# Setup of a 32-batch DiT block on one core: one block of setup before the loop against setup steps with slots of their own

## The chip, the cores and the metric

The kernel runs on one core of one Trainium2 chip. The metric is the device time of one execution in microseconds (us). Before the change three runs took 1508.64, 1509.5 and 1513.65 us, median 1509.5 us. The kernel is written for the five engines directly: TensorE (PE), VectorE (DVE), ScalarE (ACT), GpSimd (POOL) and SyncE (SP), which here issues every DMA. Each engine works through its own list of instructions in program order and waits on semaphores.

## The reference

One transformer block with modulation and cross attention, for 32 batches of 256 tokens, width 256, 16 heads of 16, context of 256 tokens, MLP width 1024, all in fp32:

```python
c_proj = silu(c) @ W_mod + b_mod                    # 32 x 1536, once for all batches
shift_a, scale_a, gate_a, shift_m, scale_m, gate_m = split(c_proj, 6)
qkv = (ln(x) * (1 + scale_a) + shift_a) @ W_qkv + b_qkv
x = x + gate_a * (self_attention(qkv) @ W_proj + b_proj)
x = x + cross_attention(ln(x) @ W_qc + b_qc, ln(context) @ W_kvc + b_kvc) @ W_cproj + b_cproj
h = gelu((ln(x) * (1 + scale_m) + shift_m) @ W_mlp1 + b_mlp1) @ W_mlp2 + b_mlp2
return x + gate_m * h
```

## The kernel before, in words

**Batches and slots.** The work is cut into 32 batches. A table `PLAN` (L34) gives every step of a batch a lag, a half and a slot; `moment` (L99) makes one slot number of it, less what `AHEAD` (L66) says. 32 slots are one batch in the steady state. Each engine walks through all slots in order, and in a slot it does the steps that are its own (its function `at`). The order of the instructions on an engine is therefore written out by hand; when they run is decided by semaphores alone. Slot 0 is the one in which the first row maxima of batch 0 are due: four matmuls `max_ps` (L661) on PE, one reduction `mx_self` (L1015) on DVE. Slots below 0 hold what comes before: `load_x` and `ln1` of batch 0 at slot -44, `norm1` (POOL) at -44, the turn `t1` at -32, `q` at -26, `q_hi` and `q_lo` at -24, `k` at -14, `stack_q` at -11, `stack_k` and `k_lo` at -10, `v` at -5; of batch 1 `load_x` at -11, `ln1` at -8, `norm1` at -2.

**Precision.** Weights and activations are split into two fp16 parts, hi and lo; each product is three matmuls (`three`, L346: L348, L349, L350). Hi is a copy on ACT (`split_weight` L755, instruction L759), lo is the difference on DVE (`split_weight` L893, instruction L897; for `mlp2` on POOL, L1123). For the weights that are stacked by heads the split is one instruction for each stripe: 17 for `qkv`, 9 for `kvc`, 8 for `qc`.

**Setup.** It stands ahead of the slots on every engine, in this order.

- SP (from L358): the DMAs of `cond`, `W_mod` (two halves of rows, L360 and L361), `b_mod` (L362), eight bias columns (L367), seven weights (L371: qkv, mlp1, kvc, proj, qc, cproj, mlp2), then bias rows and columns (L379 to L386). `load_x` (L407) comes in slot -44, so behind all of them.
- ACT: it waits for `cond`, `W_mod` and `b_mod` (`setup_in`), makes the exponential of `cond` (L763), then splits six weights.
- DVE: silu of `cond` (L887 to L889) and the copy cT (L891), then the lo parts of qkv, mlp1, kvc and proj, then the sum MOD = `c_proj` (L905), and only then the turned shifts and scales (L911 to L919) and the bias columns of q and k (L925).
- PE: the turn of silu (L529), six pairs of fp32 matmuls 128x512 for `c_proj` (L535), eight turns (L540), the folded bias of q and k.
- POOL: the identity, the fill of `k_stack_self` (L1115), the fill of V with ones (L1118).

`late_setup` stands at slot 0 on every engine and `last_setup` at slot 32 (`slots`, L152). Late setup: on DVE the lo parts of `qc` and `cproj`, the columns (L933 to L940), `v_bias` (L942), the columns of the MLP (L944), the folded rows (L947 to L955); on PE the matmuls between them, in `max_ps`, `o_ps` and `exp_ps`; on ACT the split of `mlp2`; on SP the rows out and back (L392 to L398), after all of it. PE's late setup starts with

```python
pe.wait_ge(w_lo_done, len(EARLY_W))   # L555
...
pe.wait_ge(dve_set, 12)
```

and ends with the second line: PE goes to slot 0 only when DVE has finished all of it. DVE's ends in the same way.

Of the kernel before, what the change touches and what calls it, by code (L numbers as in the profile page):

```python
# [89 lines left out]


# [13 lines left out]
class Timeline:  # L105


    def __init__(self, batches, kinds):
# [12 lines left out]
        assert len(self.steps) == batches * (len(PLAN) - 2 * len(kinds))  # L121
# [18 lines left out]
def block_kernel(nc, x, cond, ctx_in, W_mod, b_mod, W_qkv, b_qkv, W_proj, b_proj, W_qc, b_qc, W_kvc, b_kvc,  # L140
# [11 lines left out]
    def slots(at, late_setup, last_setup=None):  # L152

        for slot in range(line.first, line.last + 1):
            if slot == 0:
                late_setup()
            if slot == 2 * TILES and last_setup:
                last_setup()
            at(slot, lambda step: line.steps.get((step, slot)))

    with ExitStack() as stack:
# [103 lines left out]
        bias_in = sem("bias_in")  # L265
        setup_in, w_in = sem("setup_in"), [sem(f"w_in_{i}") for i in range(4)]
        w_hi_done, w_lo_done, late_in = sem("w_hi_done"), sem("w_lo_done"), sem("late_in")

        zeroed, ident_zero, ident_made, consts = sem("zeroed"), sem("ident_zero"), sem("ident_made"), sem("consts")
        pe_set, dve_set, act_set, sp_set = sem("pe_set"), sem("dve_set"), sem("act_set"), sem("sp_set")  # L270
# [23 lines left out]
        def flat(t):  # L294
# [8 lines left out]
        EARLY_W = W_ORDER[:-1]  # L303
        w_wait = {"qkv": (0, 16), "mlp1": (1, 16), "kvc": (2, 64), "proj": (2, 64), "qc": (2, 64), "cproj": (2, 64),
                  "mlp2": (3, 16)}

# [50 lines left out]
        def _(sp):  # L357
            nc.sync.dma_start(cnd, cond).then_inc(setup_in, 16)  # L358
# [3 lines left out]
            nc.sync.dma_start(b_mod_rows, bass.AP(tensor=b_mod.tensor, offset=0, ap=[[0, NB], [1, 6 * D]])  # L362
                              ).then_inc(setup_in, 16)
            for n in range(2):
                for a in range(2):
                    for c in range(C):
                        nc.sync.dma_start(b_qk_col[64 * a:64 * a + 64, n * C + c:n * C + c + 1], stacked_bias(b_qkv, n * D, a, c)  # L367
                                          ).then_inc(bias_in, 16)

            def load_weight(name):  # L370
                nc.sync.dma_start(staged[name], w_dram[name].rearrange("(k p) n -> p k n", p=P)  # L371
                                  ).then_inc(w_in[w_wait[name][0]], 16)

            for name in W_ORDER[:4]:
                load_weight(name)
            for name in W_ORDER[4:]:
                load_weight(name)
# [9 lines left out]
            sp.wait_ge(zeroed, 1)  # L387

            def late_setup():

                sp.wait_ge(dve_set, 12)
                nc.sync.dma_start(rows_a_dram[:, 0], MOD[:, 2 * D:3 * D]).then_inc(sp_set, 16)  # L392
                nc.sync.dma_start(rows_b_dram[:, 0], MOD[:, 5 * D:6 * D]).then_inc(sp_set, 16)
                nc.sync.dma_start(rows_a_dram[:, 1], gb_a).then_inc(sp_set, 16)
                nc.sync.dma_start(rows_b_dram[:, 1], gb_m).then_inc(sp_set, 16)
                nc.sync.dma_start(bc_dram, bc_row[0:1]).then_inc(sp_set, 16)
                sp.wait_ge(sp_set, 16 * 5)
                nc.sync.dma_start(bc_rows[:], bass.AP(tensor=bc_dram.tensor, offset=0, ap=[[0, P], [1, D]])).then_inc(sp_set, 16)  # L398
# [16 lines left out]
            def load_rows(b, dst, src, s):  # L415
                row = src[b.n:b.n + 1].rearrange("a r d -> a (r d)")
                nc.sync.dma_start(dst[:, b.u].rearrange("p r d -> p (r d)"), row.to_broadcast([P, 2 * D])
                                  ).then_inc(s[b.u], 16)

            def do_stack(b, n):  # L420

                kind = QKV_OF[n]
                if kind == "cross" and b.n == 0:
                    sp.wait_ge(consts, 3)
# [30 lines left out]
            def o_gather(b, kind):  # L455

                sp_wait(o_recip[kind], b.n)
                sp_wait(o_copied[kind], b.n * 4 + 4)
# [33 lines left out]
            def at(slot, due):  # L492
                if (b := due("load_x")):
                    load_x(b)
# [24 lines left out]
            slots(at, late_setup)  # L519
# [5 lines left out]
        def _(pe):  # L525
            pe.wait_ge(ident_made, 1)
# [4 lines left out]
            pe.wait_ge(dve_set, 2)  # L531
            for i in range(3):
                dst = (max_ps, max_ps, exp_ps)[i][0:NB, i % 2]
                for c in range(C):
                    mm = pe.matmul(dst, cT[:, c], (wm, wm2)[c][:, i * 512:(i + 1) * 512], start=c == 0, stop=c == C - 1)  # L535
            mm.then_inc(pe_set, 1)
            pe.wait_ge(dve_set, 3)
            for i, part in enumerate((0, 1, 3, 4)):
                for c in range(C):
                    mm = pe.transpose(dense_ps[:, 1, (2 * i + c) * NB:(2 * i + c + 1) * NB],  # L540
                                      MOD[:, part * D + c * P:part * D + (c + 1) * P], ident[0:NB, 0:NB])
            mm.then_inc(pe_set, 1)
            pe.wait_ge(dve_set, 5)
            pe.wait_ge(w_lo_done, 1)
            sh = lambda part, lo, c: shT[:, lo, 2 * part + c]
            for m in range(2 * C):
                for c in range(C):
                    w = slice(m * P, (m + 1) * P)
                    mm = three(pe, dense_ps[:, 0, m * NB:(m + 1) * NB], w_hi["qkv"][:, c, w], w_lo["qkv"][:, c, w],
                               sh(0, 0, c), sh(0, 1, c), c == 0, c == C - 1)  # L550
            mm.then_inc(pe_set, 1)
            pe.wait_ge(dve_set, 6)

            def late_setup():
                pe.wait_ge(w_lo_done, len(EARLY_W))  # L555
                for m in range(FC):
                    for c in range(C):
                        w = slice(m * P, (m + 1) * P)
                        three(pe, max_ps[:, 0, m * NB:(m + 1) * NB], w_hi["mlp1"][:, c, w], w_lo["mlp1"][:, c, w],
                              sh(1, 0, c), sh(1, 1, c), c == 0, c == C - 1)  # L560
                for c in range(C):
                    w = slice(2 * D, 3 * D)
                    mm = three(pe, max_ps[0:NB, 1, 0:D], sh(0, 0, c), sh(0, 1, c), w_hi["qkv"][:, c, w],
                               w_lo["qkv"][:, c, w], c == 0, c == C - 1)
                mm.then_inc(pe_set, 1)
                pe.wait_ge(dve_set, 8)
                for c in range(C):
                    pe.transpose(o_ps[:, 0, c * NB:(c + 1) * NB], v_bias[:, c * P:(c + 1) * P], ident[0:NB, 0:NB]
                                 ).then_inc(pe_set, 1)
                for c in range(C):  # L570
                    mm = three(pe, exp_ps[0:NB, 0, 0:D], vcT[:, 0, c], vcT[:, 1, c], w_hi["cproj"][:, c],
                               w_lo["cproj"][:, c], c == 0, c == C - 1)
                mm.then_inc(pe_set, 1)
                pe.wait_ge(dve_set, 10)
                for c in range(C):
                    mm = three(pe, exp_ps[0:NB, 1, 0:D], vbT[:, 0, c], vbT[:, 1, c], w_hi["proj"][:, c],
                               w_lo["proj"][:, c], c == 0, c == C - 1)
                mm.then_inc(pe_set, 1)
                pe.wait_ge(dve_set, 12)

            def last_setup():
                pe.wait_ge(consts, 2)
# [7 lines left out]
            def turn(b, unit, k):  # L590

                pe.wait_ge(norm_step[k], b.n * 3 + 3)
                ps = tenant(b, unit)
                for c in range(C):
# [5 lines left out]

# [611 lines left out]
```

## Time and profile before

| | |
|---|---|
| three runs, us | 1508.64, 1509.5, 1513.65 |
| the profiled execution, us | 1505.56 |
| its span, us | 1503.3 |
| mean granted TensorE clock | 0.972 |
| PE busy | 1380.9 us, 92% |
| DVE, ACT, POOL busy | 74%, 73%, 47% |
| first row maximum on DVE (slot 0) | 52.7 us |

The profiled execution took 1505.56 us for a span of 1503.3 us, so 2.3 us lie around the span. It is 3.9 us below the median of the three runs. The shares of busy time are means over the whole span; the change touches its first 55 us.

### The profile page before, as it was taken

The numbers are of one execution on the slowest core, as the hardware profiler recorded it, in microseconds if no ns is written. First come the engines' busy times: TensorE is split into PE (matmuls) and PEld (weight loads), VectorE is DVE, ScalarE is ACT, GpSimd is POOL, SyncE is SP. The second block draws the span as 40 slices with busy tenths as digits, with TensorE's granted clock in tenths as the row PEclk, the third lists the DMA queues.
The fourth block names the chain that finished last, engine by engine and source line by source line (L and its number), as shares of the span: only waits on it lengthen the run. The fifth ranks groups of instructions, "written<-read, shape, count | busy, mean of one in ns | idle before, by whom it ended". The sixth has DMA issues, their size and how long they took to land.

```text
span 1503.3 us, 39974 instructions
## 1 busy us (share of the span) xinstructions
PE 1380.9 (92%) x15090; PEld 910.1 (61%) x15090; DVE 1111.4 (74%) x1992; ACT 1094.2 (73%) x1852; POOL 705.6 (47%) x995
## 2 busy tenths in 40 slices
PE   2577899999999999999999999999999999999775
PEld 1234466666666666666666666666666666665544
DVE  4647887788777777788777788778777777775543
ACT  3244687777777888778778888778778888777551
POOL 2233344455545554455554554455554554445421
PEclk8779999999999999999999999999999999999988
DMA  5122233333323333333323323333333232322110
GB/s 178 50 72 87 88 94 96 97 106 101 99 91 99 89 97 98 96 105 105 99 91 100 91 91 101 97 100 109 96 95 97 90 96 95 99 91 67 52 50 15
DMA packets 142133, 137.97 MB, mean 92 GB/s; under 512 B 38070, under 2 KB 116567, under 8 KB 141943
## 3 DMA queue, kind: packets, MB, share of 16 engines
q1 hardware_dynamic: 141942, 135.42, 29.0%
q8 instruction: 121, 1.98, 0.6%
q14 instruction: 70, 0.57, 0.1%
HBM read 56.34 MB, written 9.55 MB: 44 GB/s over the span
## 4 chain that ended last, share of the span: by engine, by line
PE 77%; DVE 9%; DMA 4%; ACT 3%; issue 3%; POOL 2%; SPq 2%; DVEq 0%; ACTq 0%; POOLq 0%
PE dense_ps L348 15%; PE dense_ps L350 13%; PE dense_ps L349 13%; PE o_ps L696 13%; PE max_ps L661 10%; PE exp_ps L678 7%; PE dense_ps L596 4%; DVE mx_cross L1015 3%; DVE mx_self L1015 2%; DMA o_rb_cross<-r_dram_cross 2%; ACT probs L818 1%; SPq L433 1%; DMA r_dram_cross<-o_r_cross 1%; PE dense_ps L623 1%; POOL Y L1179 1%
## 5 line engine op out<-in xcount | busy, mean ns | idle before, releaser
L818 ACT ACTIVATE probs<-exp_ps 128x1024 f32<-128x1024 f32 x512 | 525.3, 1026 | 189.0 <-PE exp_ps L678 186.5
L1015 DVE TENSOR_REDUCE mx_cross<-max_ps 128x4 f32<-128x1024 f32 x256 | 313.4, 1224 | 101.8 <-PE max_ps L661 94.2
L1015 DVE TENSOR_REDUCE mx_self<-max_ps 128x4 f32<-128x1024 f32 x256 | 312.3, 1220 | 78.5 <-PE max_ps L661 76.4
L1150 POOL TENSOR_TENSOR o_n_self<-o_n_self,o_rb_self 128x512 f32<-128x512 f32 x32 | 40.5, 1266 | 292.9 <-DMA o_rb_self<-r_dram_self 292.9
L1183 POOL TENSOR_TENSOR g_split<-G,g_split 128x512 f16<-128x512 f32 x120 | 136.5, 1159 | 58.5 <-ACT g_split L807 58.5
L348 PE MATMUL dense_ps<-mlp_hi,g_split 128*128 128x256 f16 x504 | 140.2, 278 | 5.1 <-DVE g_split L1093 5.1
L348 PE MATMUL dense_ps<-xt,mlp_hi 128*128 128x256 f16 x512 | 140.8, 275 | 3.0 <-DVE xt L979 2.8
L349 PE MATMUL dense_ps<-xt,mlp_hi 128*128 128x256 f16 x512 | 140.5, 274 | 0.0
L350 PE MATMUL dense_ps<-xt,mlp_lo 128*128 128x256 f16 x512 | 140.4, 274 | 0.0
L350 PE MATMUL dense_ps<-mlp_hi,g_split 128*128 128x256 f16 x504 | 139.6, 277 | 0.0
L349 PE MATMUL dense_ps<-mlp_lo,g_split 128*128 128x256 f16 x504 | 139.5, 277 | 0.0
L696 PE MATMUL o_ps<-probs,V_self 128*32 128x256 f32 x2048 | 138.2, 388 | 0.0
L696 PE MATMUL o_ps<-probs,V_cross 128*32 128x256 f32 x2048 | 137.5, 386 | 0.2 <-ACT o_sb_cross L826 0.2
L849 ACT ACTIVATE G<-dense_ps,cols_b_all 128x256 f32<-128x256 f32 x256 | 103.6, 469 | 34.6 <-PE dense_ps L350 34.5
L661 PE MATMUL max_ps<-k_stack_self,q_stack_self 48*128 48x256 f16 x1024 | 101.6, 277 | 22.3 <-DVE mx_self L1015 17.3
L661 PE MATMUL max_ps<-k_stack_cross,q_stack_cross 48*128 48x256 f16 x1024 | 101.1, 276 | 21.5 <-DVE mx_cross L1015 19.3
L1141 POOL TENSOR_SCALAR xn<-X,nm,rs 128x256 f32<-128x256 f32 x192 | 105.6, 557 | 10.5
L1150 POOL TENSOR_TENSOR o_n_cross<-o_n_cross,o_rb_cross 128x512 f32<-128x512 f32 x31 | 39.4, 1270 | 151.1 <-DMA o_rb_cross<-r_dram_cross 151.1
L678 PE MATMUL exp_ps<-q_stack_self,k_stack_self 50*128 50x256 f16 x1024 | 100.1, 273 | 10.0 <-ACT probs L818 6.7
L678 PE MATMUL exp_ps<-q_stack_cross,k_stack_cross 50*128 50x256 f16 x1024 | 98.9, 270 | 8.3 <-ACT probs L818 7.7
L661 PEld LDWEIGHTS max_ps<-k_stack_cross,q_stack_cross 48*128 48x128 f16 x1024 | 29.4, 94 | 91.3 <-DVE mx_cross L1015 60.7
L696 PEld LDWEIGHTS o_ps<-probs,V_self 128*32 128x32 f32 x2048 | 53.7, 109 | 49.8 <-issue 28.0
(230 smaller groups left out, 3337.3 us busy)
## 6 DMA issues: line engine op xcount, KB each, us to landing
q_stack_self<-split_q SPq DMA_DIRECT2D x192, 64.0 KB, 2.6
k_stack_self<-split_k SPq DMA_DIRECT2D x192, 64.0 KB, 2.6
k_stack_cross<-split_kc SPq DMA_DIRECT2D x192, 64.0 KB, 2.6
q_stack_cross<-split_qc SPq DMA_DIRECT2D x192, 64.0 KB, 2.6
X<-in_x SPq DMA_DIRECT2D x32, 256.0 KB, 2.8
Ctx<-in_ctx SPq DMA_DIRECT2D x32, 256.0 KB, 3.2
rows_a<-rows_a_dram SPq DMA_DIRECT2D x32, 256.0 KB, 3.4
o_n_self<-o_sb_self SPq DMA_DIRECT2D x64, 128.0 KB, 2.8
```

Of the source, the lines that this page charges most:

```text
L348: eng.matmul(dst, a_hi, b_hi, start=first, stop=False)
L349: eng.matmul(dst, a_hi, b_lo, start=False, stop=False)
L350: return eng.matmul(dst, a_lo, b_hi, start=False, stop=last)
L661: mm = pe.matmul(max_ps[:, ab, qt * T:(qt + 1) * T], q_stack[kind][rows, b.u, p, qt * P:(qt + 1) * P], k_stack[kind][rows, b.u, p], start= ...
L678: mm = pe.matmul(exp_ps[:, ab, kt * T:(kt + 1) * T], k_stack[kind][rows, b.u, p, kt * P:(kt + 1) * P], q_stack[kind][rows, b.u, p], start= ...
L696: mm = pe.matmul(o_ps[32 * j:32 * j + 32, 0, (g % 2) * T:(g % 2 + 1) * T], V[kind][:, b.u, kt, 4 * g + j], probs[:, tile % 8, kt * T:(kt + ...
L818: nc.scalar.activation(probs[:, t % 8:t % 8 + 2], exp_ps[:], ACT.Exp).then_inc(exp_taken[kind], 2)
L849: last = nc.scalar.activation(G[:, f], bank(f"mlp1_{i}")[:, m * T:(m + 1) * T], ACT.Gelu_apprx_tanh, bias=cols_b_all[:, b.n, C + f:C + f + 1])
L1015: nc.vector.tensor_reduce(mx[kind][:, :, :, t // 2].rearrange("p q a -> p a q"), max_ps[:].rearrange("p a (q k) -> p a q k", q=2), AX_X, A ...
L1141: last = nc.gpsimd.tensor_scalar(xn[k][:, t], src[:, t], nm[k][:, t:t + 1], rs[k][:, t:t + 1], ALU.add, ALU.mult)
L1150: nc.gpsimd.tensor_tensor(o_n[kind][:], o_n[kind][:], o_rb[kind][:], ALU.mult).then_inc(o_mult[kind], 1)
L1183: nc.gpsimd.tensor_tensor(g_split[:, 1, 2 * i:2 * i + 2], G[:, 2 * i:2 * i + 2], g_split[:, 0, 2 * i:2 * i + 2], ALU.subtract).then_inc(g_ ...
```

## The change

Each setup step gets a name and a slot in a table `FOLD`, and each engine does it inside `at` like a step of a batch. `late_setup` and `last_setup` are gone. The diff, cut to its core:

```diff
+FOLD = {"mod_0": -43, "mod_0_out": -43, "mod_0_turn": -42, "mod_0_split": -42, "hi_qkv": -44, "lo_qkv": -41,
+        "q_bias": -30, "q_bias_out": -30, "hi_mlp1": -25, "hi_kvc": -13, "hi_proj": -12, "hi_qc": -12, "hi_cproj": -12, "hi_mlp2": -4,
+        "lo_mlp1": -10, "lo_kvc": -9, "lo_proj": -8, "lo_qc": -8, "lo_cproj": -7, "lo_mlp2": 1,
+        "mod_rest": -41, "mod_add": -29, "mod_turn": -25, "shift_split": -23, "columns": -9,
+        "shift": -4, "shift_out": -4, "row_v": -3, "row_v_out": -2, "row_c": -3, "row_c_out": -2, "gate": -1, "gate_out": -1,
+        "rows_out": 0, "row_back": 1, "k_ones": 33, "v_ones": -25}
@@ SP: W_mod in two parts, qkv and x early, no bias columns of q and k
-            nc.sync.dma_start(wm[:, 0:6 * D], wm_dram[:, 0]).then_inc(setup_in, 16)
-            nc.sync.dma_start(wm2[:, 0:6 * D], wm_dram[:, 1]).then_inc(setup_in, 16)
+            nc.sync.dma_start(wm[:, 0:2 * D], wm_dram[:, 0, 0:2 * D]).then_inc(mod_in, 16)
+            nc.sync.dma_start(wm2[:, 0:2 * D], wm_dram[:, 1, 0:2 * D]).then_inc(mod_in, 16)
+            load_weight("qkv")
+            nc.sync.dma_start(X[:, 0], x[0:1].rearrange("a (t p) d -> p (a t) d", p=P)).then_inc(x_in[0], 16)
             nc.sync.dma_start(b_mod_rows, bass.AP(tensor=b_mod.tensor, offset=0, ap=[[0, NB], [1, 6 * D]])
+                              ).then_inc(b_mod_in, 16)
+            nc.sync.dma_start(wm[:, 2 * D:6 * D], wm_dram[:, 0, 2 * D:6 * D]).then_inc(mod_rest_in, 16)
+            nc.sync.dma_start(wm2[:, 2 * D:6 * D], wm_dram[:, 1, 2 * D:6 * D]).then_inc(mod_rest_in, 16)
+            for name in W_ORDER[1:]:
                 load_weight(name)
-            sp.wait_ge(zeroed, 1)
@@ PE: 36 matmuls of the identity first, then steps
+            pe.wait_ge(ident_made, 2)
+            fill(o_ps[:, 0], 36)
             pe.wait_ge(dve_set, 1)
...
+            def mod_0():
+                pe.wait_ge(dve_set, 2)
+                pe.wait_ge(mod_in, 16 * 2)
+                for c in range(C):
+                    mm = pe.matmul(max_ps[0:NB, 0], cT[:, c], (wm, wm2)[c][:, 0:2 * D], start=c == 0, stop=c == C - 1)
+                mm.then_inc(pe_set, 1)
+            def mod_rest():
+                pe.wait_ge(mod_rest_in, 16 * 2)
...
+            def row_c():
+                pe.wait_ge(dve_set, dve_value["columns"])
+                pe.wait_ge(dve_set, dve_value["shift_out"])
+                pe.wait_ge(w_lo_done, w_turn("cproj"))
...
-                pe.wait_ge(dve_set, 12)
@@ PE: waits with their first reader (batch 0 only)
+                    pe.wait_ge(w_lo_done, w_turn(name))      # features_out, tokens_out
+                        pe.wait_ge(mlp2_lo_done, 1)          # mlp2_part
+                        pe.wait_ge(dve_set, 3)               # maxima: MOD's first part was in max_ps
+                        pe.wait_ge(dve_set, dve_value["row_c_out"])   # exps
+                        pe.wait_ge(dve_set, dve_value["gate_out"])    # values
@@ ACT
-            act.wait_ge(setup_in, 16 * 4)
+            act.wait_ge(cond_in, 16)
             nc.scalar.activation(cexp, cnd, ACT.Exp, scale=-1.0).then_inc(act_set, 1)
-            for name in EARLY_W:
-                split_weight(name)
+            for n in range(2):
+                for a in range(2):
+                    for c in range(C):
+                        nc.scalar.dma_start(b_qk_col[64 * a:64 * a + 64, n * C + c:n * C + c + 1], stacked_bias(b_qkv, n * D, a, c)
+                                            ).then_inc(bias_in, 16)
@@ DVE: the same operations, as steps mod_0_out, mod_0_split, q_bias_out, mod_add, shift_split, columns, shift_out, row_v_out, row_c_out, gate_out
-            for name in EARLY_W[:4]:
-                split_weight(name)
...
+            def shift_out():
+                dve.wait_ge(late_in, 16 * 14)
+                dve.wait_ge(pe_set, pe_value["shift"])
@@ POOL
+            pool.wait_ge(dve_set, 2)
             nc.gpsimd.memset(k_stack["self"][:], SHIFT_UNIT).then_inc(zeroed, 1)
```

In a slot the setup steps stand ahead of the steps of the batches on DVE, PE, ACT and POOL. The order of the engine lists that comes out of it is, on DVE: `ln1` of batch 0, `mod_0_out`, `mod_0_split`, lo qkv, `q_bias_out`, `t1_lo`, `mod_add`, `q_lo`, `shift_split`, lo mlp1, `k_lo`, lo kvc, `columns`, lo proj, lo qc, `ln1` of batch 1, lo cproj, `shift_out`, `row_v_out`, `row_c_out`, `gate_out`, first maximum. On PE: 36 matmuls of the identity, turn of silu, `mod_0`, `mod_0_turn`, `mod_rest`, `t1`, `q_bias`, `q`, `mod_turn`, `k`, `v`, `shift`, `row_v`, `row_c`, `gate`, first maximum matmuls. On ACT: exponential, eight DMA issues, hi qkv, `t1_hi`, hi mlp1, `q_hi`, `k_hi`, hi kvc, hi proj, hi qc, hi cproj, `v_hi` with hi mlp2.

## Rows read from the trace of the kernel before

**Rows 1.** The page: the span, then PE's busy tenths in 40 equal slices.

```profile
span 1503.3 us, 39974 instructions
...
PE   2577899999999999999999999999999999999775
```

**Rows 2.** The chain of waits over the first 53 us: start, us, what.

```profile
12.53 3.83 ACT qkv_hi L759 x17
...
16.38 3.43 DVE qkv_lo L897 x17
...
19.81 2.20 DVE mlp_lo L897
...
22.01 1.96 DVE kvc_lo L897 x9
...
24.58 1.79 DVE q_stack_cross L905 x3
...
26.41 1.07 PE dense_ps L540 x8
...
27.51 0.37 DVE shT L911 x2
...
30.04 0.76 DVE stats L964 x2
...
43.85 1.33 DVE qc_lo L897 x8
...
45.18 0.61 DVE cproj_lo L897
...
51.68 0.42 DVE XC L955
...
52.71 1.24 DVE mx_self L1015
```

**Rows 3.** DMA issues of the first 60 us: KB each, median us to landing.

```profile
V_self<-in_L_xcond_W_mod SPq DMA_DIRECT2D x1, 768.0 KB, 4.6
...
V_cross<-in_L_xcond_W_mod SPq DMA_DIRECT2D x1, 768.0 KB, 6.5
...
probs<-in_L_xcond_b_mod SPq DMA_DIRECT2D x1, 192.0 KB, 7.3
...
k_stack_cross<-in_cond SPq DMA_DIRECT2D x1, 32.0 KB, 1.7
```

**Rows 4.** The timeline of SP's queue: start, us.

```profile
0.72 0.40 SPq L358
...
2.58 5.13 SPq L367 DMA_DIRECT2D b_qk_col<-in_L_xcond_b_qkv  x8
...
11.81 3.75 SPq L379 DMA_DIRECT2D X<-in_L_xcond_b_qkv  x1
...
24.54 0.98 SPq L407 DMA_DIRECT2D X<-in_x  x2
```

**Rows 5.** Busy time by stage: us, PE, PEld, DVE, ACT, POOL busy, PEclk, DMA share, GB/s.

```profile
12.50:20.00 7.50, 7.16 (x14) 1.73 (x14) 3.85 (x19) 6.83 (x24) 0.00 (x0) 1.00 1.06 377
...
52.00:113.00 61.00, 36.38 (x306) 18.82 (x308) 31.63 (x55) 20.86 (x33) 16.59 (x24) 0.75 0.20 63
```

**Rows 6.** The timeline of PE and ACT: start, us.

```profile
13.20 1.92 PE L535 MATMUL max_ps<-V_self,cT 128*32 128x512 f32 x2 [0.32 <-DVE cT L891]
...
33.65 1.09 PE L596 MATMUL dense_ps<-ident,xn 128*128 128x128 f32 x4 [4.52 <-POOL xn L1141]
...
36.76 0.37 PE L348 MATMUL dense_ps<-xt,qkv_hi 128*128 128x256 f16 x1 [2.02 <-DVE xt L979]
...
39.51 0.84 ACT L790 ACTIVATE split_q<-dense_ps,cols_a_all 128x256 f16<-128x256 f32 x2 [3.81 <-PE dense_ps L350]
...
40.08 0.27 PE L349 MATMUL dense_ps<-xt,qkv_hi 128*128 128x256 f16 x1
```

**Rows 7.** The timeline of POOL in the late setup.

```profile
46.98 4.06 POOL L1123 TENSOR_TENSOR mlp_lo<-g_split,mlp_hi 128x2048 f16<-128x2048 f32 x1 [0.21 <-ACT mlp_hi L759]
```

More of the change, by code:

```diff
@@ L525, in _, with fill @@
         def _(pe):
-            pe.wait_ge(ident_made, 1)
+            def fill(bank, count):
+                for _ in range(count):
+                    pe.matmul(bank[:, 0:P], ident16[:], ident16[:], start=True, stop=True)
+            pe.wait_ge(ident_made, 2)
+            fill(o_ps[:, 0], 36)
             pe.wait_ge(dve_set, 1)
@@ L537, in _ @@
[L537 to L550, printed above, removed]
@@ L556, in late_setup, with mod_turn, shift @@
+            def mod_turn():
+                pe.wait_ge(dve_set, dve_value["mod_add"])
+                for i in range(2 * C):
+                    mm = pe.transpose(o_ps[:, 0, i * NB:(i + 1) * NB], MOD[:, 3 * D + i * P:3 * D + (i + 1) * P],
+                                      ident[0:NB, 0:NB])
+                mm.then_inc(pe_set, 1)
+            def shift():
+                pe.wait_ge(dve_set, dve_value["shift_split"])
+                pe.wait_ge(w_lo_done, w_turn("mlp1"))
                 for m in range(FC):
@@ L702, in at @@
             def at(slot, due):
+                if due("mod_0"):
+                    mod_0()
+                if due("mod_0_turn"):
+                    mod_0_turn()
+                if due("q_bias"):
+                    q_bias()
+                if due("mod_rest"):
+                    mod_rest()
+                if due("mod_turn"):
+                    mod_turn()
+                if due("shift"):
+                    shift()
+                if due("row_v"):
+                    row_v()
+                if due("row_c"):
+                    row_c()
+                if due("gate"):
+                    gate()
                 if (m := line.max.get(slot)):
@@ L809, in at @@
             def at(slot, due):
+                for name in W_ORDER:
+                    if due(f"hi_{name}"):
+                        split_weight(name)
                 if (e := line.exp.get(slot)):
@@ new lines, in q_bias_out @@
+            def q_bias_out():
+                dve.wait_ge(bias_in, 16 * 8)
+                then(nc.vector.tensor_scalar_mul(b_qk_col[:, 0:C], b_qk_col[:, 0:C], HD ** -0.5))
+                dve.wait_ge(pe_set, pe_value["q_bias"])
+                for m in range(2 * C):
+                    last = nc.vector.tensor_scalar_add(cols_a_all[:, :, m], dense_ps[:, 0, m * NB:(m + 1) * NB],
+                                                       b_qk_col[:, m:m + 1])
+                last.then_inc(dve_set, 1)
```

302 lines of the change are left out of this document (188 added, 114 removed).

## The prediction

> **What bounds the kernel now.** I read the page first. PE is busy in nine tenths or more of each slice from the sixth to the 37th, and only in the first few does it stand half idle [rows 1]. So the loop is bound by PE, a start that is shorter moves the whole loop forward, and nothing in the loop gives it back unless it is a thing of fixed time. Then I read the chain of waits over the first 53 us [rows 2]. What the reader is to see there: the first maximum on DVE, which opens the loop (slot 0), stands at 52.7 us, and before it the chain is a string of setup. ACT's split of `qkv` starts only at 12.5; then DVE makes four lo parts in a row (16.4 to 24.6) although q needs the first alone; then comes the sum MOD (1.8), turns and columns, and only at 30.0 the statistics of the first x, which SP asked for at 24.5, behind all other loads [rows 4]. From 43.9 on it is the late setup on DVE, 8.2 us from the lo part of `qc` to the last folded row at 52.1. In the stage after that, 52 to 113 us, PE is busy for 36.4 of 61 us at a granted clock of 0.75 [rows 5], a mixture of both levels. A difference within 0.3% (4.5 us) can't be told from no change in a measurement of this kernel.
>
> **The change, part by part.** I follow the new order of the lists; times are from the start of the span.
>
> *Start.* ACT waits for `cond` alone. It is asked for at 0.7 and takes 1.7 to land [rows 3, 4], so at 2.4; its exponential and then eight DMA issues follow on ACT. SP's eight took 5.1 us, 0.64 each [rows 4]; I take that for ACT too. From below an issue costs ACT nothing; from above the nearest row is the 3.75 us that one issue took with the queue full (L379). I take 0.64, since the eight are the same DMAs. ACT is free at 2.4 + 0.4 + 5.1 = 7.9. By then `qkv` has landed: both halves of `W_mod`, 1.5 MB, were in at 1.6 + 6.5 = 8.1 before [rows 3], and now the two small parts of it, `qkv` and x are 1.5 MB together. Hi qkv takes 3.8 to 11.8, lo qkv 3.4 to 15.2 [rows 2]. In that time, at no cost: x's statistics, `mod_0`, its turn and split on DVE and PE (done near 11.5), the fill of `k_stack_self` on POOL, which now waits for the silu, and `norm1` behind it (near 12.5). If that cover were gone, `t1` would be late by the same time.
>
> *mod_rest.* PE stands at it until the rest of `W_mod` is in. `b_mod` landed at 2.1 + 7.3 = 9.4 after 1.7 MB [rows 3], and the same bytes stand before it now; the 1.0 MB of the rest at 377 GB/s [rows 5] is 2.8 more, 12.2. Four fp32 matmuls of 512 columns, two in 1.9 at the slow start [rows 6], make 3.4: 15.6 (all at the fast level 1.8: 14.0). Queued behind them on PE are `t1`, `q_bias` and all of q. `t1` takes 1.1, 16.7; `q_bias` some 0.7 more, then DVE's columns, five small instructions at 0.19 each [rows 2], 18.4; `t1_lo` 0.8: **19.2, where q can start. Before it was 36.8** [rows 6].
>
> *Queries and keys.* The twelve matmuls of q took 2.75 before the first half was released at 39.5 [rows 6], so 21.9. q_hi and q_lo, 0.84 each, 23.6. `mod_add` (1.8) lies in DVE's wait for q. `shift_split`, three or four small instructions, 0.8: 24.4. Lo mlp1 2.2 [rows 2]: 26.6; hi mlp1 was made by ACT while it waited for q. `k_lo` 27.5. Meanwhile PE: four turns 0.5, k at most 2.75, 25.2; ACT: k_hi 26.0, hi kvc, nine of the stripes of which 17 take 3.8, 2.0: 28.0. That is the one place where DVE waits for ACT (0.5). The stack DMAs of q and k, twelve issues of 0.64, start when the long list of loads is through. SP's stall of 3.75 [rows 4] will come earlier now, with `W_mod`'s rest and six weights queued; with it SP is through the list and x of batch 1 by 23 to 28, and the last stack DMA has landed by 31 to 38. This is just covered by DVE's work.
>
> *Folds and late splits.* All on DVE: lo kvc 2.0 to 30.0; lo proj, lo qc, lo cproj 0.6 + 1.3 + 0.6 = 2.5; the statistics of batch 1, 1.0 with the aggregate; then what the late setup did behind lo cproj, 45.8 to 52.1, 6.3 us with its waits for PE [rows 2]; one of these (for `shift`) falls away, and `row_c` now stands behind `shift_out`, which brings about as much. 30.0 + 2.5 + 1.0 + 6.3 = 39.8. PE has issued the first maximum matmuls by then, so DVE's first maximum is at **40.1 us instead of 52.7: 12.6 us**.
>
> *Behind slot 0.* POOL's lo mlp2 takes 4.1 [rows 7]; it is hidden in the stretch in which POOL has nothing else. SP's rows out and back stand in the same slots as before and wait for the same `gate_out`. The new waits with the first readers are met long before. The removed ends of late setup on PE and DVE free nothing more, since the maximum waits for DVE in any case. The 36 filling matmuls lie in PE's wait for the silu (2 to 5.7).
>
> The sum: 1505.6 - 12.5 = 1493.1 for an execution like the profiled one. That one lies 3.9 under the median of the runs shown, 1509.5; on the median it is **1497.0 us**.
>
> Where the clock enters: the matmuls of q took 0.37 us each or more at its start, and from 40.1 on 0.27 [rows 6], and the sum takes the slow pace for both groups and for `mod_rest`. The Trainium skill ("TensorE: Matmul & The Clock Gate", section "HAM oscillation — how this bites in real kernels") says that PE falls back to half its clock when it waits between groups; so by the page the sum would stay, and the fill, whose warmth is lost in the wait for the rest of `W_mod`, would bring nothing. If the clock stayed up, the rows would give 1.6 for `mod_rest` and 1.4 for each of q and k, some 4 us more.
>
> The same for the move of eight DMAs to ACT. SP gave 5.1 us to them and `qkv` went out behind them [rows 4]. The skill ("DMA: Bandwidth & Descriptors", section "Issuing engines are not separate DMA queues") says that another issuing engine saves only the sequencer's time of issue, no transfer time; by it the 5.1 us are only moved to ACT, in front of hi qkv. In the sum they stand there.
>
> **The rivals.**
>
> *A, the forecast: the loop starts 9 to 16 us earlier and keeps it.* 0.67.
>
> *B, the clock takes it back.* The stage 52 to 113 us is worked at a mean clock of 0.75 with PE 36.4 busy [rows 5]. If the new start leaves PE in the low level for most of it, PE's time there grows to as much as 36.4 x 0.75 / 0.5 = 54.6, 18 us more; about half of that on the path is 9. The gain would be 3.5: 1506. For it: the clock does change several times in that stage, and what it does depends on how PE was used before. Against: the order of work behind slot 0 is the same, so its gaps are too; and the same sum the other way, all at the high level, is 9 us less on PE. The rule of the first page named above is this mechanism. 0.13.
>
> *C, the queue of loads is late.* SP's stall lasts until the last weight is in; the bias rows land late, `columns` waits for them on DVE, with everything behind it, and so does the first maximum for k's stack DMAs. With SP through its list at 28 (the late end of the range above), the rows land about 31, where `columns` is due at 30.0, and k's stack at 38; each stall more of 3.75 goes through in full. Loss 2 to 5. The gain would be 8: 1501.5. 0.15.
>
> *D, slower: the issues on ACT.* If an issue on ACT costs what the full queue cost SP, 3.75 each, ACT starts hi qkv at 2.8 + 30 = 32.8 instead of 7.9. Everything from lo qkv on hangs on it, 24.9 later; less the 12.5 that is 12.4 over before: 1522. It decides from 0.64 + 12.5 / 8 = 2.2 us per issue. For it: ACT's issues come while SP fills the same engines. Against: SP's own eight took 0.64 each with 1.7 MB in flight. 0.05. That the change doesn't do what it says is ruled out by the lists: late setup has no place left.
>
> **How the numbers follow.** The likeliest case is A on the median, 1497.0. Low end: 16 us from 1505.6, with the clock up and a run like the profiled one, 1489. High end: the gain of B on the median is 1506, 1507. A, C and half of B lie in it. Faster by over 0.3% (under 1505.0): A, C and some of B, 0.84. Same: most of B and what A loses between, 0.11. Slower: D, 0.05.
>
> **What would show it.** In the new profile: ACT's split of `qkv` near 8 and DVE's near 12; `mod_rest` ending at 14 to 16; q's first matmul near 19; DVE with few gaps from 24 on, and the first `mx_self` near 40; the stage of 61 us behind it [rows 5] as long and as busy as before within 2 us, and the end as much earlier as the first maximum. Wrong would be: eight issues on ACT longer than 2 us each (D); the first maximum near 40 and the next batches stretched with a clock near 0.5 (B); DVE waiting for a DMA in `columns` (C).

## The result, and the profile of the changed kernel

The changed kernel takes 1501.39 us, the median of five runs (1497.05 to 1503.25); before stands at 1509.52. The ratio is 0.9932 with a 95% interval of 0.9913 to 0.995. The forecast was 1497.0 us, a ratio of 0.9917; the range of 1489 to 1507 holds the time. It is faster by 8.1 us where 12.5 were forecast. The direction is right, and so is the cause, a loop that starts earlier; several terms of the sum are not.

The profiled execution took 1501.39 us for a span of 1498.9. The page, for [rows 1]:

```profile
span 1498.9 us, 40065 instructions
...
PE   5566899999999999999999999999999999998876
...
PEclk8589999999999999999999999999999999999987
```

The chain of waits over the first 60 us (start, us, what), for [rows 2]:

```profile
4.06 10.64 DMA V_cross<-in_L_xcond_W_mod
14.75 5.65 PE exp_ps L593 x8
20.40 0.59 PE dense_ps L655 x4
21.69 0.75 DVE cols_a_all L1021 x4
22.44 0.77 DVE xt L1099 x2
...
27.05 2.20 DVE mlp_lo L999
29.25 0.79 DVE split_k L1107 x2
30.04 1.95 DVE kvc_lo L999 x9
...
38.22 0.12 DVE vbT L1064
...
39.59 3.53 DVE XC L1071
43.12 0.34 DVE XC L1075
...
43.83 1.22 DVE mx_self L1158
```

The first maximum stands at 43.83 us instead of 52.71 [rows 2]: 8.9 earlier, not 12.6, and just short of case A's 9 to 16. Up to q (the matmuls of q begin at 23.3) the chain is one load and one piece of PE's work: the second half of the rest of `W_mod`, which lands at 14.7, and `mod_rest` on PE (L593), 5.65 us. Then comes DVE's row of splits and folds, and in it one instruction of 3.53 us (L1071).

Loads of the first 20 us (KB, us to landing), for [rows 3]:

```profile
probs<-in_L_xcond_W_qkv SPq DMA_DIRECT2D x1, 768.0 KB, 8.3
V_self<-in_L_xcond_W_mod SPq DMA_DIRECT2D x1, 512.0 KB, 8.2
V_cross<-in_L_xcond_W_mod SPq DMA_DIRECT2D x1, 512.0 KB, 10.6
...
b_qk_col<-in_L_xcond_b_qkv ACTq DMA_DIRECT2D x8, 0.2 KB, 7.3
```

The timeline of ACT, SP, PE, POOL and DVE, for [rows 4, 6, 7]:

```profile
2.42 6.77 ACTq L856 DMA_DIRECT2D b_qk_col<-in_L_xcond_b_qkv  x8
10.38 3.83 ACT L848 ACTIVATE qkv_hi<-probs 128x64 f16<-128x64 f32 x17 [7.54 <-DMA probs<-in_L_xcond_W_qkv]
4.06 1.14 SPq L392 DMA_DIRECT2D V_cross<-in_L_xcond_W_mod  x1
14.75 1.92 PE L593 MATMUL exp_ps<-V_self,cT 128*32 128x512 f32 x2 [1.24 <-DMA V_cross<-in_L_xcond_W_mod]
16.46 1.91 PE L593 MATMUL exp_ps<-V_cross,cT 128*32 128x512 f32 x2
...
38.77 4.07 POOL L1269 TENSOR_TENSOR mlp_lo<-g_split,mlp_hi 128x2048 f16<-128x2048 f32 x1
39.52 3.60 DVE L1071 TENSOR_TENSOR XC<-q_stack_cross,X 32x256 f32<-32x256 f32 x1
```

The last two rows belong together. POOL's lo part of `mlp2` runs from 38.77 to 42.84; DVE's product of two tiles in SBUF begins at 39.52 and ends at 43.12, just behind it. The same product before the change:

```profile
50.31 1.00 DVE L952 TENSOR_TENSOR XC<-q_stack_cross,X 32x256 f32<-32x256 f32 x1
```

It took 1.00 us there, and POOL's instruction [rows 7] ended at 51.04, 0.27 us ahead of its end. So before, the same collision cost the product 0.6; now it costs it 3.2. What that is worth on the first maximum, the experiments show.

Busy time by stage, for [rows 5]:

```profile
12.50:20.00 7.50, 5.88 (x12) 1.61 (x12) 4.56 (x22) 1.70 (x7) 1.97 (x4) 0.58 1.07 366
43.80:104.80 61.00, 36.50 (x296) 18.46 (x296) 31.47 (x55) 19.29 (x30) 16.07 (x23) 0.70 0.21 62
43.83:52.83 9.00, 4.64 (x26) 2.13 (x28) 5.88 (x8) 0.84 (x2) 0.00 (x0) 0.50 0.39 89
```

Behind slot 0 the same 61 us run at a granted clock of 0.70 instead of 0.75, and in the first 9 us of them PE had the low level (0.50) throughout.

### The profile page after: what moved, and what is told of

Its sections match the earlier page's. It is cut to its first block, busy times and chain, and to the rows that moved or that the text cites. A ratio compares the mean times of both kernels' runs of the same rounds, so it can differ in the third digit from the quotient of the medians.

```text
span 1498.9 us, 40065 instructions
## 1 busy us (share of the span) xinstructions
PE 1387.1 (93%) x15126; PEld 914.1 (61%) x15126; DVE 1114.8 (74%) x1992; ACT 1094.6 (73%) x1852; POOL 708.1 (47%) x995
## 4 chain that ended last, share of the span: by engine, by line
PE 73%; DVE 9%; DMA 7%; issue 3%; POOL 3%; ACT 3%; SPq 2%; DVEq 0%; ACTq 0%; POOLq 0%
PE dense_ps L369 15%; PE dense_ps L371 13%; PE dense_ps L370 13%; PE o_ps L767 12%; PE max_ps L728 10%; PE exp_ps L747 7%; PE dense_ps L655 4%; DVE mx_cross L1158 4%; DMA o_rb_cross<-r_dram_cross 4%; DVE mx_self L1158 1%; DMA r_dram_cross<-o_r_cross 1%; ACT probs L914 1%; POOL o_n_cross L1303 1%; POOL Y L1332 1%; DMA V_cross<-in_L_xcond_W_mod 1%
## 5 line engine op out<-in xcount | busy, mean ns | idle before, releaser
L728 PE MATMUL max_ps<-k_stack_self,q_stack_self 48*128 48x256 f16 x1024 | 102.3, 279 | 22.6 <-DVE mx_self L1158 19.2
L728 PE MATMUL max_ps<-k_stack_cross,q_stack_cross 48*128 48x256 f16 x1024 | 100.8, 275 | 22.4 <-DVE mx_cross L1158 19.8
L747 PE MATMUL exp_ps<-q_stack_cross,k_stack_cross 50*128 50x256 f16 x1024 | 98.7, 270 | 12.9 <-ACT probs L914 12.2
L767 PEld LDWEIGHTS o_ps<-probs,V_cross 128*32 128x32 f32 x2048 | 53.7, 109 | 49.5 <-issue 27.4
```

The source lines that it names most:

```text
L728: mm = pe.matmul(max_ps[:, ab, qt * T:(qt + 1) * T], q_stack[kind][rows, b.u, p, qt * P:(qt + 1) * P], k_stack[kind][rows, b.u, p], start= ...
L747: mm = pe.matmul(exp_ps[:, ab, kt * T:(kt + 1) * T], k_stack[kind][rows, b.u, p, kt * P:(kt + 1) * P], q_stack[kind][rows, b.u, p], start= ...
L767: mm = pe.matmul(o_ps[32 * j:32 * j + 32, 0, (g % 2) * T:(g % 2 + 1) * T], V[kind][:, b.u, kt, 4 * g + j], probs[:, tile % 8, kt * T:(kt + ...
```

## The experiments

Where nothing else is said, an edit is against the changed kernel, and its first maximum is compared with 43.83 us. The experiments ahead of "The three together" and those with fills on POOL's wait or on the change have one timed run each, so they are read by their profiles and not by their times (1496.05 us for POOL's split behind the folds, 1498.87 for the product ahead, 1502.51 for the fill left out and 1505.69 for the columns on SP, beside 1509.72 for before; 1500.84 for `W_mod` whole and 1501.90 for the late columns, beside 1505.33).

### POOL's split behind the folds

```diff
+                pool.wait_ge(dve_set, dve_value["gate_out"])
                 nc.gpsimd.tensor_tensor(w_lo["mlp2"][:], staged["mlp2"], w_hi["mlp2"][:], ALU.subtract
```

> POOL's split of mlp2 waits for the last folded row; DVE's product stays where it was. Theory (DVE waited for POOL's instruction): the product takes 0.7 us or less, POOL's split starts at 40 to 41 us and still takes 4.1 us, the first maximum comes at 40.7 to 41.2 us. The maxima read PSUM and were not held up beside POOL, so none of them grows over 1.25 us. Rival (a cause in DVE's own row): 3.6 us again and the first maximum near 43.8, with POOL's split now 3 us later as well.

The timeline of DVE and POOL:

```profile
38.88 0.41 DVE L1070 TENSOR_TENSOR XC<-exp_ps,X 32x256 f32<-32x256 f32 x1 [1.21 <-PE exp_ps L371]
39.22 0.40 DVE L1071 TENSOR_TENSOR XC<-q_stack_cross,X 32x256 f32<-32x256 f32 x1
40.16 0.41 DVE L1075 TENSOR_TENSOR XC<-o_ps,X 32x256 f32<-32x256 f32 x1 [0.54 <-PE o_ps L371]
...
40.94 1.21 DVE L1158 TENSOR_REDUCE mx_self<-max_ps 128x4 f32<-128x1024 f32 x1
...
41.16 4.05 POOL L1270 TENSOR_TENSOR mlp_lo<-g_split,mlp_hi 128x2048 f16<-128x2048 f32 x1 [3.29 <-DVE XC L1076]
```

The product takes 0.40 us instead of 3.60 with its operands and place unchanged, and the first maximum comes at 40.94. The theory holds: DVE had waited for POOL. The maxima beside POOL's 4.05 us still take 1.21 to 1.23.

The 2.9 us between 43.83 and 40.94 are not POOL's alone. In this execution the rest of `W_mod` was in at 14.5 instead of 14.7, `mod_rest` took 4.93 us instead of 5.65, and `k_lo` ended at 29.12 instead of 30.04, all of it ahead of the edit. From the end of `k_lo` on, the profiles can be compared whatever their start was:

| profiles | end of `k_lo` to first maximum, us |
|---|---|
| POOL beside the folds, product in its place: six profiles of the kernels below | 13.76 to 13.79 |
| product moved ahead | 13.30 |
| POOL behind the folds: five profiles of the kernels below | 11.82 to 11.84 |

(The six are the change, the change again, the fill left out, the bias columns on SP, the columns late and `W_mod` whole; the change with fills behind slot 0 has 13.78 as well. The five are the two with POOL's split alone behind, the one with fills on top of it, the warm version and the full one.) So the collision costs the first maximum 2.0 us. The product loses 3.2, but without it DVE waits for PE instead, 1.21 us for `row_c` where it had been 0.59, and 0.54 for the row of `gate`: PE makes both at the low clock there.

### The product moved ahead instead

```diff
+                nc.vector.tensor_tensor(gb_m, MOD[:, 5 * D:6 * D], b_rows["mlp2"], ALU.mult)    # in columns()
-                nc.vector.tensor_tensor(gb_m, MOD[:, 5 * D:6 * D], b_rows["mlp2"], ALU.mult).then_inc(dve_set, 1)
```

> The product of the gate row and the mlp2 bias row on DVE (32x256, both inputs in SBUF, L1071 of the changed kernel, 3.60 us there against 1.00 us before) is moved ahead of the columns, near 32 us, where POOL is idle. Theory (DVE's product waits for POOL's 4.07 us split of mlp2, which began 0.75 us earlier, and ends 0.28 us behind it): it takes 0.4 to 0.7 us in its new place, nothing takes 3 us in the old one, and the first maximum comes at 40.7 to 41.2 us instead of 43.83. Rival (the product is slow by itself, or something else holds DVE near 39.5 us): it takes 3 us or more in the new place too, or another instruction near 39.5 does, and the first maximum stays near 43.8.

```profile
32.67 0.40 DVE L1043 TENSOR_TENSOR XC<-q_stack_cross,X 32x256 f32<-32x256 f32 x1
...
40.87 0.41 DVE L1071 TENSOR_TENSOR XC<-exp_ps,X 32x256 f32<-32x256 f32 x1 [1.21 <-PE exp_ps L371]
42.15 0.41 DVE L1075 TENSOR_TENSOR XC<-o_ps,X 32x256 f32<-32x256 f32 x1 [0.87 <-PE o_ps L371]
42.60 1.58 DVE L1076 TENSOR_TENSOR XC<-XC,q_stack_cross 32x256 f32<-32x256 f32 x1
44.10 1.21 DVE L1158 TENSOR_REDUCE mx_self<-max_ps 128x4 f32<-128x1024 f32 x1
...
39.84 4.06 POOL L1269 TENSOR_TENSOR mlp_lo<-g_split,mlp_hi 128x2048 f16<-128x2048 f32 x1
```

Half a miss. The product took 0.40 us in its new place, as the theory says, but the first maximum stayed at 44.10. The next instruction with both inputs in SBUF, the product for `gb_a` (L1076, 0.41 in the experiment above), took the blow: 1.58 us, up to POOL's end at 43.90. The sums on either side of it (L1071, L1075) read PSUM and took 0.41 with POOL busy. Also, this execution was late before the edit could count (`k_lo` ended at 30.80 instead of 30.04), and DVE waited 1.21 us for `row_c`, which PE made at the low clock. From the end of `k_lo` it is 13.30 us instead of 13.79: the edit brought 0.5.

### The fill at the start left out

```diff
-            fill(o_ps[:, 0], 36)
```

> The 36 filling matmuls of the identity at PE's start are left out. Theory (they lie in a wait and what they warm is lost in the wait for the rest of W_mod): the rest of W_mod starts on PE at 14.7 and takes 5.6 us within 0.5, the first maximum stays at 43.8 within 0.5 us. Rival (they carry the clock to the rest of W_mod or to q): these take up to 1.2 us more, and so does the first maximum.

```profile
14.69 6.17 PE exp_ps L592 x8
...
44.29 1.22 DVE mx_self L1157
```

`mod_rest` took 6.17 us instead of 5.65 and the first maximum came at 44.29, 0.46 later. That is just inside the bound set for the theory. It is also inside what profiles with the fill show among themselves: `mod_rest` took 4.93 to 6.29 us in the nine in which it waits for the late part of `W_mod`. No effect of the fill is shown.

### The bias columns back on SP

```diff
-                        nc.scalar.dma_start(b_qk_col[...], stacked_bias(b_qkv, n * D, a, c)).then_inc(bias_in, 16)
+                        nc.sync.dma_start(b_qk_col[...], stacked_bias(b_qkv, n * D, a, c)).then_inc(bias_in, 16)
```

> The eight bias columns of q and k go back to SP's queue, behind the rest of W_mod and ahead of the six weights; ACT issues nothing. Theory (on ACT they are covered by the wait for the rest of W_mod on PE): ACT's split of qkv starts 1 to 2.5 us earlier than 10.4, which brings nothing to q (23.3 within 0.5), but SP's list ends 5 us later, so the bias rows and the stack DMAs are late: columns wait about 3 us on DVE and the first maximum comes at 46 to 48 us. Rival (the eight issues on ACT, 6.77 us, are what made the start late): q starts 1 us or more earlier and the first maximum comes before 43.3.

```profile
4.94 5.98 SPq L396 DMA_DIRECT2D b_qk_col<-in_L_xcond_b_qkv  x8
...
14.71 4.35 SPq L401 DMA_DIRECT2D X<-in_L_xcond_b_qkv  x1
...
28.77 3.84 SPq L459 DMA_DIRECT2D q_stack_self<-split_q  x6
32.71 3.75 SPq L459 DMA_DIRECT2D k_stack_self<-split_k  x6
...
10.62 3.82 ACT L853 ACTIVATE qkv_hi<-probs 128x64 f16<-128x64 f32 x17 [7.68 <-DMA probs<-in_L_xcond_W_qkv]
```

Neither was right. ACT's split of `qkv` did not start earlier (10.62 against 10.38): with ACT free at 2.9 it waited for the load. And SP's list ended only 0.9 us later, since of SP's two long issues in the changed kernel (4.67 us for the last weight, 3.90 for the first bias row) only one was left, 4.35; SP has to wait for the loads in any case. `mod_rest` was over at 21.1 instead of 20.4, the first maximum at 44.55. So the price of the eight issues on ACT, 6.77 us, lies beside the load of `qkv`, and moving them changes less than 1 us, which is no more than executions with an unchanged start differ by.

### The bias columns behind the split of qkv

```diff
                         split_weight(name)
+                        if name == "qkv":
+                            bias_columns()          # the eight issues, in ACT's list
```

> ACT issues the eight bias columns of q and k (4-byte pieces) behind its split of qkv instead of ahead of it. Theory one (the 4-byte pieces slow the large loads): qkv lands by 8 to 9 us instead of 10.4 and the second half of the rest of W_mod by 12.5 to 13.5 instead of 14.7. Theory two (the loads are slower because of their own shapes, narrow rows and a row read by 32 partitions): qkv at 10.4 and the rest at 14.7 as before, within 0.5 us. In both the columns land late and q does not come earlier than 23.

```profile
probs<-in_L_xcond_W_qkv SPq DMA_DIRECT2D x1, 768.0 KB, 7.1
V_self<-in_L_xcond_W_mod SPq DMA_DIRECT2D x1, 512.0 KB, 7.7
V_cross<-in_L_xcond_W_mod SPq DMA_DIRECT2D x1, 512.0 KB, 9.1
```

`qkv` landed 7.1 us after its issue at 2.1 instead of 8.3, and the last part of `W_mod` 9.1 after 4.1 instead of 10.6: at 9.2 and 13.2. That lies on theory one's side, with `qkv` 0.2 short of its bound. The 4-byte pieces do slow the large loads, by 1.2 to 1.5 us. The profile with fills behind slot 0 (below) has the start of the changed kernel and ran on the chip of this one: there it was 8.5 and 11.2, so 1.4 and 2.1. All eight profiles in which ACT issues the pieces first and `W_mod` comes in parts lie at 7.7 to 8.5 us for `qkv` and 10.0 to 11.4 for the last part. The bill came on the other side: the columns landed at 20.5, q began at 23.6 and the first maximum came at 45.31. The forecast's 12.2 us for the rest of `W_mod` was still 1 us too early. The pieces were not all out of its way: ACT's queue issued five of them from 10.3 to 13.0, while the split was still running. How much of the 1 us is theirs stays open.

### W_mod whole, the modulation in one go

```diff
-            nc.sync.dma_start(wm[:, 0:2 * D], wm_dram[:, 0, 0:2 * D]).then_inc(mod_in, 16)
+            nc.sync.dma_start(wm[:, 0:6 * D], wm_dram[:, 0]).then_inc(mod_in, 16)      # wm2 likewise, the rest's loads go
-        "mod_rest": -41, ... "lo_qkv": -41
+        "mod_rest": -43, ... "lo_qkv": -42
```

> W_mod is loaded whole again, ahead of qkv, and PE makes the rest of the modulation right behind its first part, ahead of the turn; the lo part of qkv stands ahead of DVE's mod_0_split. Theory (q hangs on the rest of W_mod, which lands at 14.7 us and takes PE 5.65): both halves land near 8 us, the rest of the modulation is over by 14 to 16 us instead of 20.4, q's first matmul comes at 20.5 to 21.5 instead of 23.3, and the first maximum at 41 to 42.5 instead of 43.83. Rival (t1 and q hang on the lo part of qkv and on x as much): q not before 22.8, first maximum not before 43.3.

```profile
2.10 8.26 DMA probs<-in_L_xcond_W_qkv
10.39 3.85 ACT qkv_hi L845 x17
14.27 3.66 DVE qkv_lo L996 x17
...
24.91 0.85 ACT split_q L876 x2
...
43.80 1.22 DVE mx_self L1155
```

The rest of the modulation was over at 14.7, as expected, and q began at 22.1, 1.2 earlier but 0.6 short of the window: now `qkv`'s load and its two splits are the chain. The 1.2 us were gone at once. q's matmuls took 0.21 us from start to start (12 in 2.7) where the changed kernel has 0.11 (12 in 1.4), so q_hi began at 24.91 in both, and the first maximum is the same, 43.80. In the changed kernel, PE is busy with `mod_rest` right ahead of q, and the granted clock is 1.00 from 20 to 26 us; here PE had waited from 15.1 to 18.6.

### The three together, and the change again

The warm version has POOL's wait, `W_mod` whole, and

```diff
+                fill(o_ps[:, 0], 30)        # behind mod_0_turn
+                fill(o_ps[:, 0], 14)        # behind q_bias
```

> The change as it is, timed beside the kernel before on one chip with the two below. Its first maximum comes 8.9 us earlier than before's 52.7 in the profile, and the stages behind it (to the first maximum of batch 2: 62.7 and 61.0 us; to that of batch 4: 134.9 both) are alike. So 7 to 10 us less than before.

> The change with POOL's split of mlp2 behind the last folded row. Theory: it keeps the 2.9 us that its first maximum is earlier, so 10 to 13 us less than before and 2 to 5 us less than the change as it is. Rival (the gain is taken back behind slot 0): no difference to the change over 1 us.

> POOL's split behind the folds, W_mod whole with the rest of the modulation early, and filling matmuls of the identity on PE in its two waits before q, 30 behind the first turn and 14 behind the bias of q. Theory (with W_mod whole q's first matmul came at 22.1 instead of 23.3, but q and k ran at half the clock and took that back; PE had stood idle before them): the granted clock is 1.0 from 20 to 26 us, q's twelve matmuls take 1.4 instead of 2.75, and the first maximum comes at 39.3 to 40.2 us, 1 us earlier than with POOL's split alone. Rival (the fills don't hold the clock and lie on the path): q not before 22.5 and 2.7 long, first maximum 41 or later.

The warm version's stages, over q and k and behind its first maximum:

```profile
20.00:26.00 6.00, 4.66 (x67) 3.75 (x63) 3.90 (x14) 3.80 (x6) 0.01 (x1) 1.00 0.44 68
40.91:49.91 9.00, 5.39 (x30) 2.54 (x30) 5.88 (x8) 1.68 (x4) 4.06 (x1) 0.50 0.29 88
```

All on one chip, with before at 1507.57 us (11 runs):

| | us (range) | ratio (95%) | first maximum |
|---|---|---|---|
| the change | 1500.01 (1496.6 to 1501.62) | 0.9945 (0.9925 to 0.9965) | 43.88 |
| POOL behind | 1493.91 (1492.12 to 1498.28) | 0.9916 (0.9894 to 0.9939) | 41.95 |
| whole, POOL behind, warm | 1492.94 (1490.69 to 1497.19) | 0.9904 (0.9884 to 0.9924) | 40.91 |

The change repeats. POOL's wait brings 6.1 us in the medians, more than the 2 to 5 expected and more than the 1.9 of its first maximum here. The warm version had the clock at 1.00 from 20 to 26 us, q began at 22.4 and its twelve matmuls ran at 0.11 us from start to start, so here the fills held the clock. The first maximum at 40.91 is 0.7 later than expected, but 1.0 ahead of the version above on the same chip, which is the step that the theory gave. The time can't be told from that of the version above.

### The clock behind slot 0

The distance between first maxima (batch 0 to batch 2, batch 0 to batch 4) shows what happens behind the first one:

| profile | first maximum | clock, first 9 us behind it | to that of batch 2 | to that of batch 4 |
|---|---|---|---|---|
| before | 52.71 | 0.62 | 60.95 | 134.94 |
| the change | 43.83 | 0.50 | 62.68 | 134.94 |
| the change again | 43.88 | 0.50 | 62.45 | 137.06 |
| fill left out | 44.29 | 0.50 | 62.46 | 136.70 |
| product ahead | 44.10 | 0.81 | 59.69 | 132.65 |
| POOL behind | 40.94 | 0.80 | 59.95 | 132.45 |
| POOL behind, second profile | 41.95 | 0.80 | 59.87 | 132.36 |
| whole, POOL behind, warm | 40.91 | 0.50 | 63.20 | 134.70 |
| W_mod whole | 43.80 | 0.61 | 61.41 | 134.31 |
| columns late | 45.31 | 0.58 | 61.27 | 134.25 |
| bias columns on SP | 44.55 | 0.50 | 62.62 | 138.66 |
| POOL behind, fills behind slot 0 | 43.12 | 0.54 | 59.85 | 132.65 |
| the change, fills behind slot 0 | 43.27 | 0.50 | 62.22 | 135.35 |
| whole, POOL behind, warm, fills behind slot 0 | 40.30 | 0.81 | 60.29 | 131.31 |

Each first maximum is the start of the first `mx_self` instruction, each clock that of the stage table over the 9 us behind it. Of the profiles without fills behind slot 0, all with 0.50 there need 62.4 us or more to batch 2, those with 0.8 need 60.0 or less, and those near 0.6 stand between. The last three rows are runs with such fills. The version with POOL behind and six filling matmuls behind each maximum of batch 0, eight in each of slots 17 to 22,

```diff
                     maxima(*m)
+                    if m[0] == "self" and m[1].n == 0 and m[2] >= 2:
+                        fill(o_ps[:, 0], 6)
+                if 17 <= slot <= 22:
+                    fill(o_ps[:, 0], 8)
```

was tried as well:

> On top of the kernel with POOL's split behind the folds: PE gets six filling matmuls of the identity behind each but the first maximum of batch 0, and eight in each of slots 17 to 22, where it waits for DVE. Theory (the second batch's groups run at half the clock because PE waits there, and that costs time on the path): the granted clock is near 1.0 between 42 and 72 us instead of 0.7, twelve-matmul groups there take 1.3 instead of 2.6 us, and the distance from the first maximum of batch 0 to that of batch 2 falls from 60.0 us to 56 to 58. Rival (the groups lie beside DVE's and ACT's work): the clock rises and the distance stays within 1 us of 60.0, or grows by the fills.

The clock was 0.54 in the first 9 us, 0.69 over the first 18 and 0.98 from 18 to 31; the distance was 59.85, where it had been 59.95. So the clock rose only from 18 us on, and in the first 9 us it was lower with the fills than without (0.80). The distance is the rival's, and the row breaks the order of the table: a clock near 0.5 in the first 9 us with a distance under 60. Its one time was 1499.81 us, beside 1505.33 for before. Its first maximum came at 43.12 although the start is that of the version with 40.94: the rest of `W_mod` was in at 15.3 and `mod_rest` took 6.29 us. So much does the start differ between executions. The same fills were then tried on the two that had 0.50:

> The version with W_mod whole, the two fills before q and POOL's split behind the folds, plus six filling matmuls of the identity on PE behind each maximum of batch 0 but the first and eight in each of slots 17 to 22. In the version without them the granted clock was 0.50 in the first 9 us behind slot 0 and 0.56 from 18 to 31 us, and the first maximum of batch 2 came 63.2 us behind that of batch 0; in the profiles with 0.8 in the first 9 us it came 59.7 to 60.0 us behind. Theory (the clock behind slot 0 sets that distance): the clock is over 0.65 over the first 18 us and over 0.9 from 18 to 31, the distance falls to 59.5 to 61, and the time by 1 to 4 us below 1493. Rival (the distance comes from what precedes slot 0): the clock rises and the distance stays over 62.

> The change as it is plus the same filling matmuls behind slot 0, nothing else. In its two profiles the clock was 0.50 in the first 9 us behind slot 0 and the first maximum of batch 2 came 62.7 and 62.5 us behind that of batch 0. Theory (the clock): over 0.65 over the first 18 us, over 0.9 from 18 to 31, distance 59.5 to 61. Rival: over 62 with a higher clock.

The first 9 us behind the first maximum of the full version, then of the change with fills:

```profile
40.30:49.30 9.00, 6.00 (x53) 3.57 (x51) 6.29 (x9) 1.68 (x4) 4.06 (x1) 0.81 0.30 88
```

```profile
43.27:52.27 9.00, 6.58 (x42) 3.81 (x42) 5.55 (x7) 0.84 (x2) 0.00 (x0) 0.50 0.35 89
```

The full version had its first maximum at 40.30, batch 2's 60.29 later, at 0.81; from 18 to 31 us the clock was 0.80, not over 0.9 as expected. It took 1488.69 us (1487.48 to 1492.23), ratio 0.9886 (0.9865 to 0.9906). That is faster than the kernel before, and its interval lies apart from both of the change's; it is the lowest ratio here, but on another chip than the two versions of the table above, whose intervals it overlaps, so it is not shown to beat them.

The same run limits what was said of the fills before q. They were the same, and the clock over q and k was 0.78 instead of 1.00: `W_mod` had landed sooner, PE had nothing to do from 15.3 to 18.0 us, ahead of `t1`, and the first eight matmuls of q ran at 0.21 us from start to start.

The change with fills kept 0.50 over its first 9 us, although PE was busy in 6.58 of them, had 0.59 over the first 18 and 0.68 from 18 to 31, and the distance was 62.22: a miss. Its single time, 1494.39, lies below all of the change's, but one run is no verdict.

So low clock and long distance go together in most rows, but not in the one with POOL behind and fills. The fills alone do not set the clock at slot 0, and what does, and whether it is the clock that makes the distance, stays open.

## Why the prediction was right or wrong

**Right.** The loop is bound by PE and the start moves it: with the first maximum 8.9 us earlier, the medians differ by 8.1 us here and by 7.6 when both were run again. That the loop keeps the gain rests on these medians. The two profiled executions are only 4.2 us apart (1505.56 and 1501.39), and that of before was 3.9 under its median, so they can't show it. The order of the engines was the one written out: q behind `mod_rest`, `t1_lo` and the bias, then DVE's row, then the first maximum behind `gate_out`. Rival D fell: an issue on ACT cost 0.85 us, not 2.2. Rival C fell: SP's last stack issue was made by 35.6, and DVE did not wait for a DMA in `columns`. That its 1501.5 is nearly the measured time is chance.

**Luck.** The number is nearer than the terms. Up to q the sum was 4.1 us short and at the folds 2.0; a clock that it had too low gave 1.5 back, a wait for hi kvc that did not come 0.5, and the folds 0.3. What is left is 3.7 us of first maximum.

**The load of the start** ("By then `qkv` has landed"; "12.2"). Mis-sized: `qkv` was in at 10.4 instead of by 8, the rest of `W_mod` at 14.7. The sum let the bytes count alone; the 4-byte pieces on ACT's queue cost 1.2 to 2.1 us of it, as the run with late columns showed.

**mod_rest** ("Four fp32 matmuls of 512 columns, two in 1.9"). A row was misread. "x2" in [rows 6] are the two records of one matmul: the program issues six of them there (three groups of two), and the trace of before has 12 records, from 13.2 to 20.0. One is 1.71 us from start to start at the low clock and 0.86 at the high one, so four are 6.8 or 3.4, and 5.65 were measured. The 1.8 and 1.6 that the text gave for the fast level are too small for the same reason. Both terms together put q's start at 23.3 instead of 19.2.

**q and k at the low clock** ("the sum takes the slow pace for both groups"). They ran at the high one, 1.4 us each, behind a PE that `mod_rest` had kept busy. That is 2.7 us less of PE's time; q's half of it was on the path, so DVE's row started 2.6 late (27.0 instead of 24.4) and not 4.1. Hi kvc was no longer waited for. The text had only a fall of the clock in a wait in mind, and not the work just ahead of q. The run with `W_mod` whole shows an earlier q with its matmuls twice as long, behind a wait of 3.50 us, and the warm version on top of it an early q at the high clock.

**Folds and splits on DVE.** From the end of `k_lo` (30.04) to the first maximum 13.8 us, where the text had 12.1 from 28.0. With POOL's split out of the way it is 11.8, so the sum of this part was right within 0.3; what it lacked is the collision.

**The step that failed** is "POOL's lo mlp2 takes 4.1; it is hidden in the stretch in which POOL has nothing else". I named what POOL did beside it and not what DVE did. It cost 2.0 us of first maximum, and the row that shows it (1.00 us for a product that takes 0.40) was in the trace of before, unread. The Trainium skill ("SBUF — State Buffer", section "Who interferes with whom") says that a DVE instruction with two SBUF inputs contends with a GpSimd instruction that reads SBUF, that the order of issue decides which of the two is blocked, and that a DVE instruction with at most one SBUF input, outside the two-port modes, does not contend. The traces agree in each row: 3.60, 1.58 and 1.00 us for products of two SBUF tiles beside POOL, 0.41 for sums that read PSUM, 1.21 for maxima.

**Behind slot 0** ("in the same slots as before", the stage "as long and as busy"). Rival B has at most a small part: 62.7 instead of 61.0 us to batch 2 at a clock of 0.70 instead of 0.75, gone again at batch 4 in one profile (134.94) and 2.1 in the other. The first 9 us at 0.50 where before had 0.62 are its sign, but that the clock took the time is not shown.

## What to carry to other kernels

When work moves into a gap of one engine, look at what the neighbour does in that gap too: a long GpSimd instruction over SBUF beside a DVE instruction with two SBUF inputs is a serial chain, whoever has time to spare. Before a duration is taken from a row with "xN", check it against the program's own count of instructions. At a start with a half-idle PE, an earlier first matmul is only worth what its clock leaves; look at the granted clock of the stretch before and after, and after every move look again, since the same filling matmuls held it in one version and not in the next. Before two profiles of a start are compared, find the last point that the edit could not touch and count from there: with the same start, the first maximum moved by up to 2.2 us between executions.

## What the runs showed that was not expected

- A wait of one engine's queue (`pool.wait_ge`) at the right place brought 6.1 us in the medians, nearly as much as the whole change (7.6), with 2.0 of start and a granted clock of 0.80 instead of 0.50 in the next 9 us. Another 2.6 us were seen in the profiles by batch 2; whether the clock is their cause was not isolated.
- Eight DMAs of 256 bytes in 4-byte pieces, 2 KB together, made the large loads (2.8 MB) that ran beside them 1.2 to 2.1 us later.
- PE busy for 6.58 of 9 us got the low clock throughout in one run, and PE busy for 6.00 of 9 us had 0.81 in another: the busy share of a stretch alone does not tell its clock.
